# Logits in one piece and outputs turned by transposes in a decoder layer's attention

## What is computed

```python
x = layernorm(x + attn(x))              # 16 heads of 64, CoPE position bias
x = layernorm(x + cross(x, ctx))        # one head, 1601 context rows
x = layernorm(x + ffn(x))               # low rank 64, 1024 features, gelu

def attn(x):                            # what the change touches
    q, k, v = heads(x @ Wq), heads(x @ Wk), heads(x @ Wv)
    sim = q @ k.T / 8
    P = min(reverse_cumsum(sigmoid(sim)), 63)      # position by gates
    E = q @ pos_emb
    sim = sim + frac(P) * E[ceil(P)] + (1 - frac(P)) * E[floor(P)]
    return concat(softmax(sim) @ v) @ Wout + b_out
```

## Time and profile before

| | us |
|---|---|
| median of three runs (2296.54 to 2298.07) | 2297.18 |
| the profiled execution | 2298.53 |
| its span, first to last instruction | 2296.7 |
| PE busy | 2230.2 |
| ACT busy | 1762.8 |
| DVE busy | 1634.0 |
| POOL busy | 389.3 |
| attention part, up to about | 1860 |
| 512 maxima of DVE (L842) | 568.1 |
| 4096 transposes of PE (L640) | 567.4 |
| 512 exponentials of ACT (L507) | 566.9 |
| 1024 copies of slots by ACT (L483) | 554.2 |

### The profile page before, as it was taken

How to read it: one execution, slowest core, us unless ns; L and a number is a source line. 1 busy time by engine, 2 the same in 40 slices (tenths; PEclk the granted TensorE clock), 3 DMA queues, 4 the chain that set the end, 5 groups by cost and what they waited for, 6 DMA issues and landing times. The chain is left out here.

```text
span 2296.7 us, 53197 instructions
## 1 busy us (share of the span) xinstructions
PE 2230.2 (97%) x14577; PEld 1449.5 (63%) x14577; DVE 1634.0 (71%) x4269; ACT 1762.8 (77%) x3723; POOL 389.3 (17%) x673
## 2 busy tenths in 40 slices
PE   7999999999999999999999999999999978999997
PEld 5666666666666666666666666666665556777775
DVE  5888888888888888888888888888888801233232
ACT  5888888888888888888888888888888843454453
POOL 1111111111111111111111111111111201121211
PEclk9999999999999999999999999999999989999998
DMA  2010101010101010101010101010102021010100
GB/s 74 24 40 25 39 23 39 23 42 23 40 24 39 23 39 23 39 23 39 23 39 23 39 23 39 23 39 23 34 15 58 12 66 35 28 41 30 39 30 7
DMA packets 109392, 75.44 MB, mean 33 GB/s; under 512 B 28077, under 2 KB 105070, under 8 KB 109294
## 3 DMA queue, kind: packets, MB, share of 16 engines
q1 hardware_dynamic: 109294, 73.95, 11.5%
HBM read 14.33 MB, written 2.10 MB: 7 GB/s over the span
## 5 line engine op out<-in xcount | busy, mean ns | idle before, releaser
L842 DVE TENSOR_REDUCE mx<-Sc 128x1 f32<-128x1024 f32 (+1 forms) x512 | 568.1, 1131 | 246.9 <-PE Sc L632 246.9
L483 ACT ACTIVATE probsT<-rings 128x512 f32<-128x512 f32 x1024 | 554.2, 594 | 196.9 <-PE rings L640 196.5
L640 PEld LDWEIGHTS rings<-ident,probs 128*128 128x128 f32 x4096 | 437.8, 141 | 303.5 <-issue 103.8
L507 ACT ACTIVATE probs<-Sc,nbias 128x1024 f32<-128x1024 f32 x512 | 566.9, 1112 | 29.3 <-DVE nbias L852 29.3
L640 PE MATMUL rings<-ident,probs 128*128 128x128 f32 x4096 | 567.4, 282 | 3.0 <-ACT probs L507 2.5
L632 PE MATMUL Sc<-qk,q_now 64*128 64x512 f32 x2048 | 530.0, 615 | 14.9 <-ACT probs L507 10.5
L654 PE MATMUL out<-probsT,V_now 128*64 128x256 f32 x4096 | 498.3, 386 | 0.0
L805 DVE COPY_PREDICATED z<-mask,z 128x224 f32<-128x224 int16 (+5 forms) x768 | 393.5, 512 | 10.8
L375 POOL TENSOR_TENSOR prod<-cut,z 128x350 f32<-128x350 f32 x128 | 120.7, 943 | 1468.7 <-DVE z L817 1468.7
L654 PEld LDWEIGHTS out<-probsT,V_now 128*64 128x64 f32 x4096 | 271.4, 136 | 153.6 <-issue 42.4
L632 PEld LDWEIGHTS Sc<-qk,q_now 64*128 64x128 f32 x2048 | 177.3, 186 | 120.0 <-issue 104.9
(11 more groups left out here) (128 smaller groups left out, 2261.9 us busy)
## 6 DMA issues: line engine op xcount, KB each, us to landing
q_now<-qk SPq DMA_DIRECT2D x256, 64.0 KB, 2.0
xv<-xT SPq DMA_DIRECT2D x113, 128.0 KB, 2.2
q_far<-qk SPq DMA_DIRECT2D x256, 32.0 KB, 1.8
V_now<-V SPq DMA_DIRECT2D x16, 512.0 KB, 3.0
at<-attn SPq DMA_DIRECT2D x16, 512.0 KB, 3.2
probs<-in_x_dram SPq DMA_DIRECT2D x4, 512.0 KB, 5.5
wqk<-in_L_attn_Wq_dram SPq DMA_DIRECT2D x32, 64.0 KB, 2.0
xin<-in_x_dram SPq DMA_DIRECT2D x16, 128.0 KB, 2.8
```

Source lines behind the costliest of these rows:

```text
L483: nc.scalar.activation(probsT[:, u, 4 * s:4 * s + 4, :], ring[k % 2][:, :].rearrange("p (t q) -> p t q", q=P), ACT.Copy).then_inc(slot_out, 1)
L507: nc.scalar.activation(probs[:, u, cols], Sc[:, cols], ACT.Exp, bias=nbias[:, u:u + 1], accum_out=sums[:, u, half:half + 1]).then_inc(exp_ ...
L640: last = nc.tensor.transpose(ring[k % 2][:, j * P:(j + 1) * P], probs[:, u, (4 * s + j) * P:(4 * s + j + 1) * P], ident[:, :])
L842: nc.vector.tensor_reduce(mx[:, u, half:half + 1], Sc[:, cols], AX.X, ALU.max).then_inc(dve_unit, 1)
```

## The change

- PE's body issues both logits of unit 0 together, and late 2 and 3 after them. The wait for the last exponential of the iteration before now stands ahead of these transposes.
- ACT takes the second exponential of unit 1 directly behind the first, ahead of `empty_halves` and the projections' copies. `positions` and `distances` stand ahead of the copies of late 2 and 3, which follow together with those of last 0 to 3.
- `turns_of` makes two 128x128 transposes with the identity; the two halves of a unit stand side by side in `turns`. ACT scales the first halves into `attn` as before; DVE multiplies the second halves by 1/sum and adds them (`add_other_halves`: two scalar_tensor_tensor of 128x64 an iteration, behind the wait for ACT's scaling, ahead of unit 1's maxima).
- The matrix `fold` goes, with its set-up on POOL.

```diff
--- before.py
+++ after.py
@@ -138,7 +138,6 @@
         V = sb("V", [P, 4, NT, C])
         V_now = sb("V_now", [P, NT, C])
         halves = sb("halves", [P, 2, P])
-        fold = sb("fold", [P, C])
         sums = sb("sums", [P, 2, 2])
         rowsum = sb("rowsum", [P, 2])
         q_far = sb("q_far", [P, P])
@@ -202,6 +201,7 @@
         halves_out = sem("halves_out")
         k_near_in = sem("k_near_in")
         turned = sem("turned")
+        added = sem("added")
         scaled = sem("scaled")
         summed = sem("summed")
         dve_unit = sem("dve_unit")
@@ -350,15 +350,10 @@
 
         @block.gpsimd
         def _(pool):
-            nc.gpsimd.memset(fold[:, :], 0.0).then_inc(consts, 1)
             nc.gpsimd.memset(near_table_in[:, :, :], 0.0).then_inc(consts, 1)
-            for half in range(2):
-                pool.wait_ge(consts, 2 + half)
-                nc.gpsimd.affine_select(out=fold[:, :], in_=fold[:, :], compare_op=ALU.not_equal, fill=1.0,
-                                        base=-half * C, pattern=[[-1, C]], channel_multiplier=1).then_inc(consts, 1)
-            pool.wait_ge(consts, 4)
             for odd in range(2):
                 of_q, of_k = (slice(0, C), slice(C, P)) if odd else (slice(C, P), slice(0, C))
+                pool.wait_ge(consts, 1 + 2 * odd)
                 nc.gpsimd.memset(qk_scale[of_q, odd:odd + 1], C ** -0.5).then_inc(consts, 1)
                 nc.gpsimd.memset(qk_scale[of_k, odd:odd + 1], 1.0).then_inc(consts, 1)
 
@@ -408,7 +403,7 @@
                 act.wait_ge(slot_full, s + 1)
                 nc.scalar.activation(xT[:, s % 2, s // 2 * BANK:(s // 2 + 1) * BANK], ring[s % 2][:, :],
                                      ACT.Copy).then_inc(slot_out, 1)
-            act.wait_ge(consts, 8)
+            act.wait_ge(consts, 5)
             act.wait_ge(dve_consts, 5)
 
             def project(s, odd, base, k, alone=False):
@@ -490,7 +485,7 @@
                 if u == 0:
                     act.wait_ge(rsum_done, g + 1)
                     wait_apart(act, turned, g + 1, waited)
-                nc.scalar.activation(attn[:, t * 2 + u, bass.ds(h * C, C)], turns[:, u * C:(u + 1) * C], ACT.Copy,
+                nc.scalar.activation(attn[:, t * 2 + u, bass.ds(h * C, C)], turns[:, u * P:u * P + C], ACT.Copy,
                                      scale=rsum[:, u:u + 1]).then_inc(scaled, 1)
 
             def empty_halves(g):
@@ -510,12 +505,11 @@
             def body(g, odd, late=False, first=False, second=False, proj=True, val=True, far=True, near=True):
                 base = slots_before(g, late)
                 at = Slots()
-                if not first:
-                    transposed(0, base, at.late, (2, 3))
                 if near:
                     positions(g + 1)
                     distances(g + 1)
                 if not first:
+                    transposed(0, base, at.late, (2, 3))
                     transposed(1, base, at.last)
                 exp_half(g, 0, 0)
                 exp_half(g, 0, 1)
@@ -528,13 +522,13 @@
                     steps(g + 2)
                 transposed(0, base, at.now, (0, 1))
                 exp_half(g, 1, 0)
+                exp_half(g, 1, 1)
                 if not first:
                     empty_halves(g - 1)
                 if proj:
                     project(g + PAIRS, not odd, base, at.qk, alone=not val)
                 if val:
                     values(g, base, at.values)
-                exp_half(g, 1, 1)
 
             body(0, False, first=True)
             body(1, True, second=True)
@@ -607,7 +601,6 @@
                                             start=True, stop=True)
                 last.then_inc(near_full, 1)
 
-            pe.wait_ge(consts, 4)
             pe.wait_ge(slot_out, 8)
             for s in range(PAIRS):
                 if s == WINDOW0 + 1 or s == WINDOW1 + 1:
@@ -660,8 +653,7 @@
 
                 pe.wait_ge(halves_out, g + 1)
                 for u in range(2):
-                    last = nc.tensor.matmul(turns[:, u * C:(u + 1) * C], halves[:, u, :], fold[:, :],
-                                            start=True, stop=True)
+                    last = nc.tensor.transpose(turns[:, u * P:(u + 1) * P], halves[:, u, :], ident[:, :])
                 last.then_inc(turned, 1)
 
             def body(g, odd, par, late=False, first=False, proj=True, val=True, far=True, far_par=None,
@@ -675,13 +667,13 @@
                     wait_apart(pe, exp_done, g * 4 - 1, waited)
                 logits(par, 0, 0)
                 if not first:
-                    transposes(0, base, at.late, 2)
-                    transposes(0, base, at.late, 3)
                     wait_apart(pe, exp_done, g * 4, waited)
                 if new_keys:
                     wait_apart(pe, slot_out, base - 1, waited)
                 logits(par, 0, 1)
                 if not first:
+                    transposes(0, base, at.late, 2)
+                    transposes(0, base, at.late, 3)
                     transposes(1, base, at.last, 0)
                     transposes(1, base, at.last, 1)
                     if not second:
@@ -740,7 +732,7 @@
             transposes(1, base, at.last, 2)
             transposes(1, base, at.last, 3)
             outputs(G - 1, base, at.last, range(NT))
-            pe.wait_ge(scaled, 2 * (G - 1))
+            pe.wait_ge(added, 2 * (G - 1))
             turns_of(G - 1)
 
         @block.vector
@@ -864,6 +856,15 @@
                     wait_apart(dve, scaled, g * 2, waited)
                 nc.vector.reciprocal(rsum[:, :], rowsum[:, :]).then_inc(rsum_done, 1)
 
+            def add_other_halves(g):
+
+                h, t = g // PAIRS, g % PAIRS
+                wait_apart(dve, scaled, g * 2 + 2, waited)
+                for u in range(2):
+                    o = attn[:, t * 2 + u, bass.ds(h * C, C)]
+                    nc.vector.scalar_tensor_tensor(o, turns[:, u * P + C:(u + 1) * P], rsum[:, u:u + 1], o,
+                                                   ALU.mult, ALU.add).then_inc(added, 1)
+
             def body(g, late=False, first=False, second=False, chain=True, scan=True):
 
                 c = g + 1
@@ -876,6 +877,8 @@
                 bias(g, 0)
                 if chain:
                     first_shifts(c)
+                if not first and not second:
+                    add_other_halves(g - 2)
                 half_max(g, 1, 0)
                 half_max(g, 1, 1)
                 window(g, 1)
@@ -904,9 +907,11 @@
                 body(g, late=True)
             body(G - 2, late=True, scan=False)
             body(G - 1, late=True, chain=False, scan=False)
+            add_other_halves(G - 2)
             dve.wait_ge(rsum_done, G - 1)
             add_halves(G - 1)
             invert(G - 1)
+            add_other_halves(G - 1)
 
 
 def general_attention(nc, A):
```

## The result

The changed kernel takes 2329.11 us (median of four runs, 2326.41 to 2330.36), the kernel before 2297.04 beside it on the same chip. The ratio is 1.0136, with a 95% interval of 1.0124 to 1.0148: 32 us slower. The forecast was 2323.5 with 2290 to 2350, and "slower" at 0.75.

The account below looks back on a forecast made before the run. A loop through all engines, paced by two ring banks, bounds the kernel. Ring 15, head starts 8, late iterations 3 and end 0.5 sum to +26.5: 2323.5 us after adjusting to the median; range 2290 to 2350.

Parts of the forecast that it names:

- The ring: Two PSUM banks pace slots; outputs, counted from X (unit 1's first exponential start), come 0.09 to 0.20 later: +15 us.
- Head starts: At 15 head changes second logits wait for the query-and-key slot's copy: +0.52 us each, +8 in all.
- Late iterations: In 13 iterations without projections, outputs start at X+7.12, +0.2 us each: +3 us (1 to 4).
- Turns: Two transposes replace four records on PE: 0.22 us less, worth nothing because the next group waits for its bank.
- Logits in one piece: Unit 0's two logits pieces on PE become one, with one fewer change to transposes: -0.3 us of PE work.
- Additions: VectorE's two additions, 0.2 to 1.0 us, fit its idle 1.0 before unit 1's maxima: nothing, at most 0.1 an iteration.
- a sign against itself: Unit 1's maxima starting behind an addition without idle time would show the forecast wrong, in favour of VectorE's wait.
- The end: At the end of the attention part the last additions follow ACT's last scaling: +0.5 us (0.3 to 1.0).
- TensorE-bound rival: Ring slots turn round in PE's own 0.46 us, saving 0.52 an iteration: -57, 2240 us; chance 0.11.
- The balance: ACT reaches its first copy at X+4.1, slots are quicker, only head starts remain: 2293 to 2301 us; chance 0.13.
- VectorE's wait: Additions of 0.5 us each plus the wait delay unit 1's maxima by 0.1 to 0.3: 2336 to 2360; chance 0.05.
- The clock rival: 26 transposes in a row lower PE's clock in a third of iterations: +62, 2385 us; chance 0.09.

Follow-up runs that it names:

- e2_order: The kernel before with only the new order on PE and ACT, fold turns kept, two ring banks: 2326.9 us.
- e7_order_bank3: The kernel before with the new order and a third ring bank, last 0 still waiting for late 2's copy: 2312.6 us.
- e8_order_free: The kernel before with the new order and a third ring bank, last 0 no longer waiting for late 2's copy: 2257.9 us.
- e11_after_no_adds: The changed kernel, two banks, without VectorE's additions and the wait ahead of them (outputs incomplete): 2330.5 us.
- e9_after_free: The whole changed kernel with a third ring bank, last 0 not waiting for late 2's copy: 2273.2 us.
- e12_free_no_adds: e9_after_free without VectorE's additions (outputs incomplete): 2236.2 us.
- e4_after_bank3: The whole changed kernel with a third ring bank, last 0 still waiting for late 2's copy: 2332.3 us.

## Why the prediction was right, step by step

**The ring.** The mechanism was named in the forecast, and each of its stations is in the trace. Late 2 was put at X+3.48 and starts at 3.50. The first copy was put at X+4.22 to 4.33 and starts at 4.19, with `dist` ending and the slot's 0.69 running out at the same moment. Last 0 was to start 0.63 behind the first copy and starts 0.65 behind it. Outputs were put at X+7.24 to 7.35 and start at 7.26. The period rose by 0.13 (14.18 to 14.31) where 0.14 was taken. The third bank shows it from the other side: it takes 69 us off e2_order, and 55 of them come with a single number, the wait of last 0 (e7_order_bank3 against e8_order_free).

**Head starts.** Their second logits were put at X+3.04 and stand at 3.09; the excess over an ordinary iteration grew by 0.57 (from 0.07 to 0.64) where 0.52 was taken. 110 times 0.13 and 14 times 0.57 are 22.3; 21.4 was measured.

```profile
494.65 1.13 PE L625 MATMUL Sc<-qk,q_now 64*128 64x512 f32 x4
496.17 1.13 PE L625 MATMUL Sc<-qk,q_now 64*128 64x512 f32 x4 [0.39 <-ACT qk L413]
```

**Late iterations: right in kind, mis-sized.** The forecast took outputs at X+7.12 and +0.2 an iteration. An ordinary late iteration takes 14.31 after 13.95, +0.36. The term that failed is "slot late 2 0.96 behind the second logits": 0.96 holds for the second half of logits in one piece, but here PE is early and must wait for the second exponential in the middle. By the sum the second half starts at X+2.45 and late 2 comes 1.05 behind it. Eight records last 2.23 instead of 2.01:

```profile
1704.64 2.23 PE L625 MATMUL Sc<-qk,q_now 64*128 64x512 f32 x8 [0.16 <-ACT probs L502]
```

So late 2 comes at 1706.80, which is X+3.50 again, just as with projections, and with it the whole iteration. The other 0.05 is in the stretch from the first copy to the outputs, 3.07 for 3.02. 13 times 0.36 are 4.7 of the 7.1 measured; about 2 more is one stall for a q_now load (below), and 0.2 the head change among them.

**Turns: nothing, as forecast,** and with the cover gone their 0.18, near the 0.22 that the prediction put at that end (its 0.45 for the fold's turns held some of the bank's wait; with the bank free they take 0.39). **Logits in one piece: -0.3 on PE, as forecast,** 0.29 by the periods above; the ring hid it.

**Additions.** The forecast took nothing, and e11_after_no_adds measures nothing. But the margin was luck in part: one addition lasts 0.28 (the two 0.51, inside the 0.2 to 1.0 given), and 0.53 pass between the end of the scaling and their start, a latency that the sum did not have. They end at the moment when the maxima can start (the logits began at 1021.92, and 1.08 is also what the maxima keep without additions):

```profile
1022.51 0.51 DVE L865 SCALAR_TENSOR_TENSOR attn<-turns,rsum,attn 128x64 f32 x2 [1.50 <-ACT attn L488]
1023.00 2.17 DVE L834 TENSOR_REDUCE mx<-Sc 128x1 f32<-128x1024 f32 x2
```

These two rows are also what the prediction named as a sign against itself: unit 1's maxima starting behind an addition without idle time. The sign was there and VectorE did not bind. It is the distance from the logits to the maxima that tells (1.08 here, 1.41 in e9_after_free).

**What the sum lacked.** Its 26.5 against 31.9 (in spans and in the profiled executions' times alike): the loop's 23 became 21.4, the late 3 became 7.1. The end was taken at +0.5 and gave -0.6: before, the clock fell to 0.52 in its last transposes, and from their first group to the outputs 5.32 went by (1848.79 to 1854.11), here 3.77 (1879.48 to 1883.25) at 1.00. The start's +1.7 and the second part's +2.3 are no effect of the change as far as the profiles tell: over all fourteen of them the first mark lies anywhere from 75.7 to 79.9, and the second part, in which the kernels are alike, takes 430.2 to 433.3 from its first transposes on. (The prediction numbered the marked iterations 2 to 112; a mark stands one iteration behind the sums that it adds, so they are 3 to 113. Differences don't change.)

**The rivals.** The TensorE-bound rival is what happens with three banks, and not with two. It gave -57 us for a ring turning in PE's own time; e12_free_no_adds is at -60 of before, with the additions out of the way. That the two agree so well is partly luck: the period falls by 0.61 and not 0.52, and the 15 head changes take some of it back. The balance failed at the first copy, X+4.19 and not 4.1. VectorE's wait is refuted by e11_after_no_adds for this kernel, and with the scaling's added wait it is what limits e9_after_free. The clock rival is refuted: the run of 26 transposes in a row is granted 1.00 (busy time by stretch, columns as in the earlier trace rows).

```profile
1014.91:1018.67 3.76, 3.51 (x28) 2.74 (x26) 3.69 (x14) 3.22 (x7) 1.72 (x4) 1.00 0.12 30
1879.48:1883.25 3.77, 3.52 (x27) 2.76 (x27) 0.00 (x0) 2.79 (x6) 0.00 (x0) 1.00 0.00 0
```

The second line holds the last transposes of the attention part, whose last eight were at 0.52 before. The Trainium skill ("TensorE: Matmul & The Clock Gate", Part 4: PE-mode transpose) says that transposes don't count as TensorE activity as matmuls do. This trace doesn't bear out the outcome that I had drawn from it: in all 127 such runs the clock keeps its upper level of 2.4 GHz through them, with matmuls on either side.

The bubble itself is in the Trainium skill ("Perfetto Trace Analysis", section Optimization Strategy): the same gap again and again on the engine that should be full can mean too few PSUM buffers. Here it was 0.25, 129 times, and a third bank with its wait moved removed it (the iterations of e8_order_free and e9_after_free have none).

## What to carry to other kernels

Before transfers into few banks are put in a row, work out one bank's round (fill, copy, free: here 1.33 us, so 0.67 a slot with two banks) beside what each engine needs alone (0.46 and 0.48): work that seemed to be in the way was what hid the difference. A saving on an engine that stands in such a ring is worth nothing until the ring is widened, and then as much as the next limit leaves: the transposed turns 10 us with VectorE's additions beside them, 0.18 an iteration without. Weigh a wait by the starts of the instructions around it, not by the idle time in a bracket: here 0.42 against 0.25. When a bank is added, each wait has to be moved with it, or most of its worth is lost (14 us of 69 with one wait left behind). Then look for what is late next: instructions that fill an idle gap exactly, as the additions did, become the limit as soon as the gap closes or what they wait for comes later, here by 0.3.

## What the runs showed of the hardware

**Instructions behind a wait started later in the loop than written out.** VectorE's additions start 0.52 to 0.56 us after ScalarE's scaling ends in each of the 124 iterations that the loops cover. In iterations 126 and 127, which are written out, they start 0.14 after it (1859.91 to 1860.05, and 1873.28 + 0.53 = 1873.81 to 1873.95), as they do twice at the end of the attention part:

```profile
1873.28 0.53 ACT L488 ACTIVATE attn<-turns,rsum 128x64 f32<-128x64 f32 x2
1873.95 0.48 DVE L865 SCALAR_TENSOR_TENSOR attn<-turns,rsum,attn 128x64 f32<-128x64 f32 x2 [5.50 <-ACT attn L488]
```

In the loop the place in `attn` is worked out from the loop's register, and the wait is against one. That these take the 0.39 is likely, but neither was tried alone. The scaling of the kernels with three banks points the same way: the one wait added ahead of it goes with 1.40 to 1.45 instead of 1.09 in the loop, and with 1.12 or 1.13 in the iterations written out.

**The clock behind waits of TensorE.** Where q_now's load came late, PE stood for about two microseconds (of 1.90 us it was busy 0.01), and the logits behind that wait ran at 0.50, the level of 1.2 GHz, eight records in 3.68 us instead of 2.01:

```profile
1804.40:1806.30 1.90, 0.01 (x3) 0.03 (x1) 1.83 (x5) 1.90 (x3) 0.00 (x0) 1.00 0.24 54
1807.00:1809.00 2.00, 2.00 (x7) 0.81 (x4) 0.60 (x1) 0.92 (x2) 1.81 (x3) 0.50 0.00 0
```

The other two late loads of this kernel made PE wait 1.45 and 1.16 (until 279.38 and 1316.62), and the logits behind them ran at 1.00, eight records in 1.99. Nor did every longer wait bring the clock down. At the end of the attention part PE stood for 2.49 before and for 2.22 here, and the same transposes followed. Before, the first eight of them were granted 1.00, the next eight 0.68, and turns and last eight 0.50 to 0.52, until the matmuls of the outputs ran at 1.00 again; here all were at 1.00. What decides it these runs do not show.

Such a load came late twice in the kernel before and three times in this one (1.89 the longest), once in some 50 iterations; in e4_after_bank3 it did seven times. What delays it was not found.
